# A factorisation kernel on one core: five of seven layer-0 matmuls in rounded passes, and other places for the layer-1 halves and the X0 read

## What is computed

```python
def _cin_layer(X0, Xi, W, b):            # W: (128, 39 * Fi)
    Wr = W.reshape(H, F0_, Fi)
    return jnp.einsum('hjk,bjd,bkd->bhd', Wr, X0, Xi) + b[None, :, None]
X0 = Xi = e
for W, b in Ws:                          # three layers, H = 128
    Xi = _cin_layer(X0, Xi, W, b)
    res.append(Xi.sum(axis=2))
h = jnp.concatenate(res + [dense_ctx], axis=1)
h = jnp.maximum(h @ W_top1 + b_top1, 0.0)    # 400 -> 512
h = jnp.maximum(h @ W_top2 + b_top2, 0.0)    # 512 -> 256
y = h @ W_top3
```

## Time and profile before

| | us |
|---|---|
| runs | 677.14, 682.29, 677.56; median 677.56 |
| profiled execution, device time | 677.52 |
| its span | 675.7 |
| PE busy | 639.8 (95%) |
| DVE busy | 577.4 (85%) |
| ACT busy | 514.3 (76%) |
| POOL busy | 346.7 (51%) |

### The profile page before, as it was taken

The page is one execution under the profiler, slowest core; times in us unless marked ns, Lnnn a source line. Parts: engine busy times, 40 slices in busy tenths (PEclk is TensorE's granted clock), DMA queues, the critical chain, the costliest instruction groups (busy, mean ns, idle before and its releaser), DMA issues.

```text
span 675.7 us, 13663 instructions
## 1 busy us (share of the span) xinstructions
PE 639.8 (95%) x2489; PEld 457.9 (68%) x2489; DVE 577.4 (85%) x1240; ACT 514.3 (76%) x1676; POOL 346.7 (51%) x339
## 2 busy tenths in 40 slices
PE   0389999999999999999999999999999999999998
PEld 0166677677777777777777777777777777766473
DVE  0457898989899999989998989999999989999580
ACT  2156878888787878787878878787878887899372
POOL 6778384838474665647383847475563333220000
PEclk9989999999999999999999999999999999999999
DMA  6532723232231303131323222231313130000200
GB/s 220 137 101 57 242 65 90 53 88 53 63 78 49 93 22 91 32 97 44 88 53 89 52 73 68 56 85 30 86 29 105 31 102 16 13 16 2 62 1 0
DMA packets 42542, 46.12 MB, mean 68 GB/s; under 512 B 20704, under 2 KB 25408, under 8 KB 42377
## 3 DMA queue, kind: packets, MB, share of 16 engines
q1 hardware_dynamic: 26146, 42.28, 21.3%
q0 software_dynamic: 5120, 1.32, 2.1%
q10 hardware_dynamic: 11239, 2.05, 1.7%
HBM read 44.30 MB, written 1.31 MB: 68 GB/s over the span
## 4 chain that ended last, share of the span: by engine, by line
PE 82%; POOL 4%; DVE 4%; issue 4%; DMA 3%; SPq 1%; ACT 1%; DVEq 0%; ACTq 0%; POOLq 0%
PE acc L413 14%; PE ya L436 11%; PE ya L437 11%; PE ya L438 10%; PE yd L436 8%; PE yd L438 7%; PE yd L437 7%; PE misc L420 4%; POOL emb L339 3%; DVE chain L558 2%; DMA tiles<-x_rows 2%; PE yd L509 2%; POOL prod L266 1%; PE yd L514 1%; PE yd L518 1%
## 5 line engine op out<-in xcount | busy, mean ns | idle before, releaser
L683 ACT ACTIVATE prods<-ya,x0t 128x128 f32<-128x128 f32 x1472 | 442.5, 501 | 100.5 <-PE ya L438 100.1
L558 DVE SCALAR_TENSOR_TENSOR chain<-yd,x0t,chain 128x128 f32<-128x128 f32 x768 | 218.2, 343 | 14.4 <-PE yd L438 13.7
L436 PE MATMUL ya<-w1h,x1h 128*128 128x512 f32 (+1 forms) x384 | 206.4, 537 | 1.9 <-DVE x1l L577 1.9
L266 POOL TENSOR_TENSOR prod<-tiles,x0a 120x512 f32<-120x512 f32 x105 | 137.3, 1308 | 126.7 <-PE acc L413 113.0
L339 POOL DMA_INDIRECT emb<-in_tables,rows x160 | 159.1, 994 | 39.4 <-issue 26.1
L437 PE MATMUL ya<-w1l,x1h 128*128 128x512 f32 (+1 forms) x384 | 148.3, 386 | 0.0
L438 PE MATMUL ya<-w1h,x1l 128*128 128x512 f32 (+1 forms) x384 | 147.7, 385 | 0.0
L573 DVE TENSOR_REDUCE x2t<-prods 128x128 f32<-128x1792 f32 x64 | 129.2, 2019 | 1.5 <-DVE chain L558 0.3
L413 PE MATMUL acc<-prod,w 120*128 120x512 f32 x224 | 117.3, 608 | 10.6 <-DVE prod L266 8.8
L573 DVE TENSOR_REDUCE prods<-prods 128x128 f32<-128x1536 f32 x64 | 111.7, 1745 | 0.0
L436 PE MATMUL yd<-w1h,x1h 128*128 128x512 f32 x256 | 104.2, 407 | 1.7 <-DVE chain L558 0.7
(11 more groups left out here) (87 smaller groups left out, 409.0 us busy)
## 6 DMA issues: line engine op xcount, KB each, us to landing
tiles<-x_rows SPq DMA_DIRECT2D x236, 78.0 KB
x0a<-x_rows SPq DMA_DIRECT2D x45, 80.0 KB
emb<-in_tables,rows POOLq DMA_INDIRECT x160, 2.5
w<-in_w SPq DMA_DIRECT2D x3, 832.0 KB, 10.5
w<-in_w SPq DMA_DIRECT2D x1, 2496.0 KB, 11.4
tiles<-x_rows SPq DMA_DIRECT2D x32, 42.0 KB
x<-x_rows SPq DMA_DIRECT2D x16, 78.0 KB
x<-x_rows SPq DMA_DIRECT2D x16, 77.8 KB
```

The source lines that it names most:

```text
L266: engine.tensor_tensor(prod0[:, i % L0_PRODS, :], tiles[:, slot, :], x0a[:, :], ALU.mult).then_inc(prod0_ready, 1)
L436: pe.matmul(out, x1h[:, xs], w1h[:, cols], start=True, stop=False)
L558: dve.scalar_tensor_tensor(out, product, x, run if step else b1[:, :], ALU.mult, ALU.add).then_inc(yd_used, 1)
L683: mm = act.activation(prods[:, :, slot_of(q) + i], ya[(NA * g + k) % YA][:, i * H:(i + 1) * H], ACT.Copy, scale=turned(c)[:, g * F1 + j:g ...
```

## The change

- Layer 0: for chunks from the third on (x = 2 to 15), tiles 0 to 4 are multiplied in three rounded passes. ACT rounds the product to `prod0h` (`round_product`, at the points `HIGH_AFTER` of its order), POOL subtracts to get `prod0l` (`split_product`, one behind each next product), PE waits for that and issues three `float32r` matmuls. Tiles 5 and 6 stay as they were, and so do chunks 0 and 1. The halves of these five tiles' weights are made once at the start, high by ACT and low by DVE; PE waits for them ahead of chunk 0.
- x1h and x1l have two buffers. x1h is rounded in one piece of 512 columns by `evacuate_x1`; x1l is made in one piece behind (3, 6), no longer from x1 but from `acc0` itself, by a scalar_tensor_tensor (add the bias, subtract x1h) that reads PSUM with a stride of four elements. `split_back` is gone.
- `lay_out` is behind (2, 1) and `turn_x0` behind (3, 1) in every chunk. SP issues `load_x0` behind the seventh tile's load.
- POOL's order: gathers 1, 1, 1, 1, 1, 2, 3 after the seven tiles, block-diagonals after tiles 1, 3, 5 and, behind its gathers, 6.
- x2t has two buffers in place of four; z1 and y lie in other tensors; the larger x1h and x1l let 31 fields of layer 2 go in rounded passes in place of 27.

```diff
+DIAG_AFTER = {1: 0, 3: 1, 5: 2, 6: 3}
+GATHERS_AFTER = (1, 1, 1, 1, 1, 2, 3)
+SPLIT, SPLIT_FROM = (0, 1, 2, 3, 4), 2
+HIGH_AFTER = {0: (3, 4), 1: (0, 0), 2: (0, 5), 3: (1, 0), 4: (1, 5)}
 def lay_after(prev):
-    return (0, 1) if prev else (2, 1)
+    return (2, 1)
 def turn_after(prev):
-    return (2, 1) if prev else (3, 1)
+    return (3, 1)
...
             def load_layer0(x, nxt):
...
-                for i in range(T0 - 1):
+                for i in range(T0):
                     load_tile(sp, x, i)
                 if nxt:
                     load_x0(x + 1)
-                load_tile(sp, x, T0 - 1)
...
+            def split_product(x, i):
+                k = SPLIT.index(i)
+                pool.wait_ge(prod0_high, splits_before(x, k) + 1)
+                pool.wait_ge(prod0_ready, T0 * x + i + 1)
+                wait_done(pool, l0_done, halves_free(x, i))
+                pool.tensor_tensor(prod0l[:, k % L0_PRODS, :], prod0[:, i % L0_PRODS, :],
+                                   prod0h[:, k % L0_PRODS, :].bitcast(F32), ALU.subtract).then_inc(prod0_split, 1)
...
                 for i in range(T0):
                     if c + 1 < CHUNKS:
                         multiply0(pool, c + 1, i)
-                    if i in DIAG_AFTER:
+                        if c + 1 >= SPLIT_FROM and i - 1 in SPLIT:
+                            split_product(c + 1, i - 1)
+                    if i in DIAG_AFTER and i < T0 - 1:
                         block_diagonal(c, DIAG_AFTER[i])
...
-                    if c + 3 < CHUNKS and 2 * i < FO:
-                        gather(c + 3, range(2 * i, 2 * i + 2))
+                    if c + 3 < CHUNKS:
+                        gather(c + 3, range(sum(GATHERS_AFTER[:i]), sum(GATHERS_AFTER[:i + 1])))
+                    if i == T0 - 1:
+                        block_diagonal(c, DIAG_AFTER[i])
...
             def layer0(x, i):
...
+                if x >= SPLIT_FROM and i in SPLIT:
+                    k = SPLIT.index(i)
+                    high, low = prod0h[:, k % L0_PRODS, :], prod0l[:, k % L0_PRODS, :]
+                    pe.wait_ge(prod0_split, splits_before(x, k) + 1)
+                    pe.matmul(acc0[:, :], w0h[:, k, :], high, start=first, stop=False)
+                    pe.matmul(acc0[:, :], w0l[:, k, :], high, start=False, stop=False)
+                    pe.matmul(acc0[:, :], w0h[:, k, :], low, start=False, stop=last).then_inc(l0_done, 1)
...
+            def split_x1(c):
+                dve.wait_ge(x1h_ready, c + 1)
+                dve.scalar_tensor_tensor(halves(x1l, c), acc0[:, :].rearrange("p (n g) -> p g n", g=GROUPS), bias[:, 0:1],
+                                         halves(x1h, c).bitcast(F32), ALU.add, ALU.subtract).then_inc(x1_split, 1)
...
                             if nxt and (g, half) == (GROUPS - 1, 1):
-                                split_x1(c + 1, FRONT, x1h_front, x1_front)
-                            if (g, half) == (0, 0):
-                                split_x1(c, BACK, x1h_back, x1_back)
+                                split_x1(c + 1)
...
+            def round_product(x, i):
+                k = SPLIT.index(i)
+                act.wait_ge(prod0_ready, T0 * x + i + 1)
+                wait_done(act, l0_done, halves_free(x, i))
+                act.activation(prod0h[:, k % L0_PRODS, :], prod0[:, i % L0_PRODS, :], ACT.Copy).then_inc(prod0_high, 1)
             def chunk(c, prev, nxt, lay):
-                split_back(c)
                 for g in range(GROUPS):
                     for q in range(BLOCKS):
                         if OWNERS[q] == "A":
                             multiply(c, g, q)
+                        for i in SPLIT:
+                            if (g, q) == HIGH_AFTER[i] and (lay if i == 0 else prev and nxt):
+                                round_product(c + 1 + (i == 0), i)
```

More of the change, by code:

```diff
@@ L111, in uses_before, with splits_before, products_free, halves_free @@
     return 0 if isinstance(x, int) and x == 0 else T0 * (x - 1) + range(i, T0, ring)[-1] + 1
+def splits_before(x, k):
+    return len(SPLIT) * (x - SPLIT_FROM) + k
+def products_free(x, i):
+    if i >= L0_PRODS:
+        px, pi = x, i - L0_PRODS
+    else:
+        px, pi = x - 1, range(i, T0, L0_PRODS)[-1]
+    if px >= SPLIT_FROM and pi in SPLIT:
+        return "split", splits_before(px, SPLIT.index(pi)) + 1
+    return "plain", T0 * px + pi + 1
+def halves_free(x, i):
+    k = SPLIT.index(i)
+    if k >= L0_PRODS:
+        return T0 * x + SPLIT[k - L0_PRODS] + 1
+    return T0 * (x - 1) + SPLIT[range(k, len(SPLIT), L0_PRODS)[-1]] + 1
 def wait_done(engine, semaphore, count):
@@ L172, in build, with flat @@
         wt1d_raw, dense_raw = x0a[0:STACK, :], tiles[0:STACK, 0, :]
-        wt1d, dense = stack[:, 0, :], stack[:, 1, :]
+        wt1d, dense = prod0h[0:STACK, 0, :], prod0l[0:STACK, 0, :]
         first_split = RING * B // H
         near = F - first_split
-        split = near + COLS // H
+        split = near + 2 * COLS // H
         whole = F - split
+        def flat(x):
+            return x[:, :, :].rearrange("p i n -> p (i n)")
         def w2_halves(i):
@@ L184, in w2_halves @@
             cols = slice((i - near) * H, (i - near + 1) * H)
-            return x1h[:, cols], x1l[:, cols]
+            return flat(x1h)[:, cols], flat(x1l)[:, cols]
         def gram_halves(i):
@@ L194, in w2_pieces @@
             return ((rows[:, 0:near * H], w1h[:, first_split * H:], w1l[:, first_split * H:]),
-                    (rows[:, near * H:], x1h[:, :], x1l[:, :]))
-        h1, h2 = gram[:, 0:4, :], gram[:, 4:6, :]
+                    (rows[:, near * H:], flat(x1h), flat(x1l)))
+        y = prod0[0:1, 0, :]
+        h1, h2, z1 = gram[:, 0:4, :], gram[:, 4:6, :], gram[:, 6, :]
         scratch = nc.dram_tensor("x0_rows", (CHUNKS, FP, COLS), F32, kind="Internal").ap()
@@ L264, in multiply0 @@
             engine.wait_ge(tile_in[slot], 16 * SEGMENTS * (x * len(range(slot, T0, L0_TILES)) + i // L0_TILES + 1))
-            wait_done(engine, l0_done, uses_before(i, L0_PRODS, x))
+            kind, count = products_free(x, i)
+            wait_done(engine, prod0_split if kind == "split" else l0_done, count)
             engine.tensor_tensor(prod0[:, i % L0_PRODS, :], tiles[:, slot, :], x0a[:, :],
@@ L435, in layer1_block @@
                 xs, out = slice(g * P, (g + 1) * P), out[:, 0:len(fields) * H]
-                pe.matmul(out, x1h[:, xs], w1h[:, cols], start=True, stop=False)
-                pe.matmul(out, x1h[:, xs], w1l[:, cols], start=False, stop=False)
-                pe.matmul(out, x1l[:, xs], w1h[:, cols], start=False, stop=True).then_inc(ready, 1)
+                pe.matmul(out, x1h[:, c % 2, xs], w1h[:, cols], start=True, stop=False)
+                pe.matmul(out, x1h[:, c % 2, xs], w1l[:, cols], start=False, stop=False)
+                pe.matmul(out, x1l[:, c % 2, xs], w1h[:, cols], start=False, stop=True).then_inc(ready, 1)
             def chunk(c, prev, nxt, lay):
@@ L567, in sum_half @@
                     dve.wait_ge(sums_done, 2 * n + 1)
-                    wait_done(dve, g_done, n - GROUPS + 1)
-                    src, out = prods[:, :, S_HALF:SLOTS], x2t[:, g, :]
+                    wait_done(dve, g_done, n - 1)
+                    src, out = prods[:, :, S_HALF:SLOTS], x2t[:, g % 2, :]
                 else:
@@ L573, in sum_half, with halves @@
                 dve.tensor_reduce(out, src, AX.X, ALU.add).then_inc(sums_done, 1)
[L575 to L578, removed]
+            def halves(x, c):
+                return x[:, bass.ds(c & 1, 1), :].rearrange("p c (g n) -> p (c g) n", n=P)
+            def split_x1(c):
+                dve.wait_ge(x1h_ready, c + 1)
+                dve.scalar_tensor_tensor(halves(x1l, c), acc0[:, :].rearrange("p (n g) -> p g n", g=GROUPS), bias[:, 0:1],
+                                         halves(x1h, c).bitcast(F32), ALU.add, ALU.subtract).then_inc(x1_split, 1)
             def sum_dims(c):
-                dve.tensor_reduce(z[:, 0, bass.ds(c * CB, CB)].rearrange("p (g b) -> p g b", g=GROUPS),
+                dve.tensor_reduce(z[:, bass.ds(c * CB, CB)].rearrange("p (g b) -> p g b", g=GROUPS),
                                   x1[:, :].rearrange("p (g d b) -> p g b d", g=GROUPS, d=D), AX.X,
```

72 lines of the change are left out of this document (40 added, 32 removed).

## The result

The changed kernel takes 681.11 us (median of 20 runs, 678.95 to 682.48) against 677.73 for the kernel before (20 runs beside them): a ratio of 1.0044 [1.0034, 1.0054]. It is slower by 3.4 us, where 4.1 us faster had been forecast: within 1%, inside the range, but of the other sign. The profiled execution, of 682.02 us, lies 0.9 above that median; its span is 680.2 us, 4.5 more than before.

What follows compares the result with a forecast made beforehand. PE sets the pace, with DVE close behind as a floor. Head +0.25, chunks 0 and 1 +1.25, middle chunks -4.4, chunk 15 -0.25, tail -0.75 sum to -3.9 from 677.5: 673.6, stated as 673.5 us; range 666 to 682.

Steps and rivals of the forecast that it cites:

- Chunks 0 and 1: PE's product waits in chunk 0 go, 2.2 us gained; ACT's wait for w2-delayed tiles loses some 4.4; together +1.25.
- now w2 leaves some 1.8 us earlier and the product starts near 80.0: First product of x = 2, behind w2's load: starts near 80.0, ends at 81.3, where ACT waits to round it.
- The bound of +3.3: Upper bound for chunks 0 and 1 together, if the ya banks carry PE through nothing of ACT's standstill.
- Middle chunks: Chunks 2 to 14: each 0.34 us shorter, a new length of 36.1, -4.4 us over the thirteen.
- of 0.93 saved, 0.59 is given back: Per chunk, five split tiles save PE 0.93 us; waits for DVE return 0.40 at (0, 3), 0.19 at (1, 8).
- 0.33 for the longer piece: DVE's split_x1 behind (3, 6): 0.8 us against 0.47 now, lengthening DVE's chain to (0, 3) by 0.33.
- Head: Start of the kernel: x1h and x1l in whole pieces cost +0.25 us; w0's halves are made during waits.
- Tail: End: four full-precision fields become three passes, -0.75 us; chunk 15 separately loses a 0.28 piece, -0.25.
- A, PE gets all of it: Rival: DVE's slack lets PE keep 0.93 us a chunk, 665.8 us; chance 0.25 with what lies between.
- B, the dear stride: Rival: DVE's strided PSUM read costs 1.16 us, so no chunk gains, 678.0 us, no change; chance 0.15.
- C as a steady state: Rival: tile 0 comes late every chunk, behind X0's reading on SP; ACT waits, 693 us at 17 us; chance 0.10.
- C's milder case, 682.7: Rival C with 16.2 us from layout to the product's end: PE loses 0.7 us a chunk, total 682.7.

Runs made afterwards that it cites:

- a_w2late: The changed kernel with w2's load moved behind the tile loads of x = 2, ahead of the reading of X0 for x = 3: 671.99 us, 0.9919.
- a_nosplit: The changed kernel with all seven tiles in full precision, without the roundings and subtractions of products: 682.21 us, 1.0076.
- a_back: The changed kernel with layout and turning of X0 back at (0, 1) and (2, 1): 677.29 us, 1.0000.
- a_ez_gathers: The changed kernel with w2's load later, split_x1 behind (3, 3), dimension sum in group 2, and gathers two behind each of the first five tiles: 675.64 us, 0.9981.
- a_w2_early: The changed kernel with w2's load behind the tile loads of x = 2 and split_x1 moved from behind (3, 6) to behind (3, 3): 665.00 us, 0.9835.
- a_w2_early_z: The changed kernel with w2's load later, split_x1 behind (3, 3), and the sum over dimensions moved from group 1 to 2: 658.71 us, 0.9723.
- a_ez_nosplit: The changed kernel with w2's load later, split_x1 behind (3, 3), dimension sum in group 2, and all seven tiles in full precision: 665.78 us, 0.9831.

## Why the prediction was wrong

**Chunks 0 and 1, +4.86 for +1.25.** The mechanism was right, and a_w2late with a_nosplit shows it from both sides. Its size was off in two terms. The product's end, forecast for 81.3, came at 84.16. The step that failed is "now w2 leaves some 1.8 us earlier and the product starts near 80.0": w2 left 0.5 earlier than before, not 1.8 (the later head is 1.1 of that), and the product began 15.6 us after it, not 14.0 as in the earlier trace rows. w2 itself took 12.8 us to land (11.4 before), and x0a's three issues stretched to 2.28. What lengthened them stays open. The profile of a_back has the same loads in the same order, x0a issued 1.95 us behind w2 as here, and its product comes near the forecast's time:

```profile
65.85 0.36 SPq L347 DMA_DIRECT2D w<-in_w  x1
...
79.13 1.27 POOL L301 TENSOR_TENSOR prod<-tiles,x0a 120x512 f32<-120x512 f32 x1 [7.03 <-issue]
```

There it began 13.3 us behind w2, and in a_nosplit 12.7 (66.42 to 79.14). So a part of this term belongs to the profiled execution. From the product's end to PE's restart it was 1.9 (1.8 forecast), and the banks held until 80.1 (78.7), so that 5.9 in place of 4.4 was lost. The second term was missing, put at nothing: the lower clock behind the gap, 2.0. The bound of +3.3 was too low too, since it held neither. Chunk 0's -2.07 for -2.2 was right, and a_ez_gathers shows its cause; that it agrees to 0.1 is luck, since chunk 0 took 35.82 to 37.45 in the profiles with that gather order.

**Middle chunks, -0.06 each for -0.34.** The step "of 0.93 saved, 0.59 is given back" failed in small pieces, all on one side. The saving is 5 x 0.17 = 0.85. The wait at (0, 3) is 0.71 (0.64), at (1, 8) 0.52 (0.47), and a third of 0.09 that I had not seen stands at (0, 7), where the gram product waits for DVE's x2t. The waits of before were 0.24 and 0.28, so 0.71 + 0.52 + 0.09 - 0.24 - 0.28 = 0.80 is given back, and 0.85 - 0.80 = 0.05 is left; the chunks show 0.08. The term was the difference of two near sums, taken thirteen times: 0.02 a tile, 0.07, 0.05 and 0.09 make 0.3 a chunk, and 3.6 us in all. In the 0.64 one term was small, DVE's wait for (3, 6), 0.54 of idle time for 0.4, and one was right by luck: 0.33 for the longer piece set a duration (0.8) against a distance of starts (0.47). By starts it is 0.20 longer, and 0.12 came from its later begin. The mechanism, DVE's chain, is shown by a_back (0.20), a_w2_early (0.64) and a_w2_early_z (0.40).

**Head, +1.1 for +0.25.** The eight other profiles of versions of the changed kernel place the first third pass at 39.92 to 40.86, three of the kernel before and its versions at 40.45 to 40.75. So the change does not lengthen the head, and the 1.1 is this execution's; what sets it stays open.

**Tail.** -0.7 for -0.75, as four full-precision fields became three passes. Chunk 15 did not gain its 0.25 (31.91 for 31.85 from its first third pass to its last): the piece of 0.28 at its head is gone, and what took its place isn't shown.

**Rivals.** A, PE gets all of it: false for the changed kernel, but nearly what two moved DVE instructions made of it (35.36 a chunk, where A had 35.6; the waits of the kernel before went too). Its argument, DVE's idle time of 2 us a chunk, was sound; the idle time just stood in the wrong places. B, the dear stride, is false: 751 ns against 693 for a contiguous tensor_tensor in SBUF. Thereby this kernel does not bear out the PSUM rule of the Trainium skill ("Advanced Engine Details and Errata", PSUM Cachelines) for a read by DVE; of matmuls, which that section names, nothing is shown. C as a steady state is false: from layout (434.10) to the product's end (446.66) it took 12.6 us in chunk 10 (12.7 forecast), and ACT's rounding began 1.4 later, without a wait. Its wait came true once, in chunk 1, by w2, which its "for it" named, and cost 7.6 us. The 216 ns of the Trainium skill ("TensorE: Matmul & The Clock Gate", Back-to-back issue gap), given there for the isolated case, would have made the saving larger still; the passes start 0.23 apart here too. C's milder case, 682.7, lay just outside the range that was said to take it in.

## What to carry to other kernels

- Ask for the slack of the second engine place by place, along its own order, and not from its busy share: here DVE had 2 us of idle time a chunk, and 7 us of the whole hung on whether one instruction of 0.75 us stood in front of a late block or in that gap.
- When an in-order engine gets a new wait, look at its first occurrence as well as at its steady state. A one-off transfer in the queue that feeds it can be harmless before and on the critical path after, and the clock adds to what a standstill costs.
- Where the difference of two near sums decides the sign of a forecast, both signs get a real chance.

## What the runs showed of the hardware

- A standstill of PE of 5.9 us was followed by 4.3 us at a granted clock of 0.50, with passes 0.42 to 0.43 apart for 0.23. In a_back one of 4.9 us was followed by the same level. By the mean granted clock of each run, it followed in 18 of the 20 runs of the changed kernel and in all ten of a_back.
- The first eight or so passes of layer 1 run at 0.50 in ten of the twelve profiles (at 41.00 to 44.00 the kernel before was granted 0.60), but in a_w2_early and a_ez_nosplit in none, and these have a chunk 0 of 35.82 where a_w2late has 36.92. It is a part of the variation between executions of one kernel.
- DVE's scalar_tensor_tensor that reads PSUM with a stride of four took 8% more than its contiguous tensor_tensor in SBUF (751 to 693 ns). The sum over dimensions, a reduce with a stride of eight in SBUF, took 1.11 to 1.18 us for as many elements; whether the stride or the reduce makes it dear isn't shown.
- A rounding of the 120-partition product by ACT took 673 ns against 633 for x1h of as many columns.
